# A decoder layer on one Trainium2 core: both folds of cross-attention on parts of the TensorE array, folded keys in two buffers, preparation steps at new places

## The chip, the cores and the metric

The kernel runs on 1 core of one Trainium2 chip. The time is that of one execution on the device, in microseconds (us); three runs of the kernel before gave 1259.86, 1261.22 and 1261.81, a median of 1261.22.

## What is computed

Sixteen sequences (batches) of 512 tokens with 256 channels go through three blocks, each followed by a layer norm of the sum with its input: a linear attention with 16 heads (state = product of two key-value sums), a cross-attention with 16 heads of 64 to 64 context tokens, and a mixture of 8 experts. The second is the one that the change is in:

```python
q = x @ Wq.T
k, v = jnp.split(context @ Wkv.T, 2, axis=-1)
sim = jnp.einsum('bhid,bhjd->bhij', heads(q), heads(k)) * SCALE
attn = jax.nn.softmax(where(mask, sim, max_neg), axis=-1)
out = jnp.einsum('bhij,bhjd->bhid', attn, heads(v))
return merged(out) @ Wout.T + b_out
```

## The kernel before

Each engine runs a program of its own, written out by hand, and they meet at semaphores. A setup computes K and V of all batches and stores them to DRAM. Then a loop goes over the batches (`it`), each in four **slots** of 128 tokens (`pe_slot`, `act_slot`, `dve_slot`, `pool_slot`, `sp_slot`). The iterations run from -2 to 16, so that a batch's inputs are prepared ahead. After the loop come the experts.

Wq is not applied to the tokens: it is folded into the keys, a = Wq.T k ("folded keys", preps A0 to A3, line 440), and Wout into the values, b = v Wout.T ("folded values", preps B0 to B3). In a slot TensorE forms the scores `sim` = t a in two halves of 8 heads, turns the probabilities of the tile before (`pt`, two halves, `pe_pT`), turns the next tokens (`tr`), forms `zb` of the linear attention (`pe_z`), and `ob` = pT b in two halves (`pe_pB`), each behind the low parts `pT_lo` of that half of the turned probabilities. VectorE takes the maximum of each half (`dve_max`), subtracts it (`dve_shift`), ScalarE takes the exponential, VectorE the sum `zsum`, and GpSimd multiplies by its reciprocal.

A product that must be exact is made of three matmuls (lines 137 to 139): each operand is split into a high part, copied by ScalarE in a rounded format (fp32r), and the rest, subtracted by VectorE. An fp32 operand that isn't split goes through TensorE as two matmul instructions in the trace, called passes here (line 440: 16 products a batch are 32 instructions). Before, the folded keys are one such fp32 product per head pair, 128 rows by 128 columns, in which K of the two heads lies on the diagonal of a tile with zeros beside it (`kraw`); the folded values are three matmuls on `vraw`, laid out likewise, whose high part ScalarE makes (line 665) and whose rest GpSimd makes (line 943).

The **preps** of later batches (G and GT: the tokens' Gram matrix and its turned part; B; T1, T0, R, ST: the state of the linear attention; A; SB, SW: its folded weights; Q0, Q1: queries) are steps of TensorE, then ScalarE, then VectorE. The table `ORDER` says in which slot and at which numbered **place** within it each of these three engines does its part. Preps write alternately to two PSUM banks (`pws`); before TensorE starts one, it waits until the one before it on the same bank was taken (`before_on_bank`), and until its operands were (`OPERANDS`: GT reads what ScalarE copied of G). ST is a step of 32 small fp32 products on four tiles of 32x32 of the array (line 416). Places of TensorE: 1 after the first half of `sim`, 2 after the second, 3 after the first half of `pt`, 4 after `tr`, 5 after `zb`, 6 after the second half of `pt`, 7 after the first half of `ob`, 8 after the second.

SP issues the DMAs: K and V of the next batch (`load_kv`, two DMAs each), the mask row into the folded keys, the inputs, and the stores.

## Time and profile before

| what | us |
|---|---|
| profiled execution: its own time | 1261.79 |
| its span, first to last instruction | 1260.1 |
| TensorE busy (matmul) | 1219.2 |
| VectorE busy | 868.0 |
| GpSimd busy | 623.7 |
| ScalarE busy | 567.2 |
| median of three runs | 1261.22 |

The span is that of one execution under the profiler. A busy TensorE counts a matmul from its start to its modelled end, which overlaps the next; the step from start to start is what one costs in a row of them. The granted clock of TensorE is 0.997 of full speed on average. The setup takes about the first 75 us; the `sim` products of the first batch start at 104.52, those of the last batch at 849.41.

### The profile page before, as it was taken

To read this page: it belongs to the slowest core of one execution; us is meant where nothing else is said; L and a number is where in the kernel's file an instruction comes from. 1 tells how busy PE (TensorE), PEld (TensorE's weight loads), DVE (VectorE), ACT (ScalarE), POOL (GpSimd) and SP (SyncE) were. 2 spreads that over 40 slices of the span, in tenths; PEclk is the share of its full clock that TensorE was granted. 3 is DMA by queue.
4 is the path that set the end of the run, shared out by engine and by line. 5 is a ranking of instruction groups with operands and counts; after the bars stand their busy time and mean duration, and the time that the engine had idled before them with its cause. 6 is when DMAs were issued, how large, how long until landed. Compare 5 with 4: busy or idle time off the path is not lost.

```text
span 1260.1 us, 24107 instructions
## 1 busy us (share of the span) xinstructions
PE 1219.2 (97%) x8848; PEld 1100.2 (87%) x8848; DVE 868.0 (69%) x1694; ACT 567.2 (45%) x1117; POOL 623.7 (50%) x986
## 2 busy tenths in 40 slices
PE   8979999999999999999999999988999999999998
PEld 7868889898898898988988989887798899899888
DVE  5557888888888888888888888887533323322435
ACT  2144556555546465556465655555423312421420
POOL 3245766766756767567567575665322112202201
PEclk9999999999999999999999999999999999999999
DMA  9820111102111111111111211220221021022001
GB/s 275 222 74 19 43 35 51 51 26 60 39 39 44 35 51 52 31 56 43 35 49 29 58 45 31 84 81 26 69 92 57 12 67 68 1 68 68 1 1 35
DMA packets 117912, 69.88 MB, mean 55 GB/s; under 512 B 74658, under 2 KB 115363, under 8 KB 117796
## 3 DMA queue, kind: packets, MB, share of 16 engines
q1 hardware_dynamic: 115764, 67.67, 18.3%
q8 instruction: 73, 1.20, 0.4%
q10 hardware_dynamic: 2032, 0.66, 0.2%
q14 instruction: 43, 0.35, 0.1%
HBM read 42.09 MB, written 26.22 MB: 54 GB/s over the span
## 4 chain that ended last, share of the span: by engine, by line
PE 79%; DVE 9%; issue 2%; POOL 1%; ACT 1%; POOLq 0%; DVEq 0%
PE ob L137 7%; PE ob L138 6%; PE ob L139 6%; PE sim L137 6%; PE sim L138 6%; PE sim L139 6%; PE pw L440 4%; PE pw L137 3%; PE pw L138 3%; PE pw L139 3%; PE pt L489 3%; PE pw L390 3%; PE pt L139 2%; PE pt L138 2%; PE pt L137 2%; DVE prob L848 2%
## 5 line engine op out<-in xcount | busy, mean ns | idle before, releaser
L1595 POOL TENSOR_TENSOR w_lo<-w_raw,w_hi 128x2048 fp32r<-128x2048 f32 x16 | 73.7, 4609 | 222.5 <-ACT w_hi L1535 169.3
L137 PE MATMUL ob<-b_hi,pT_hi 128*128 128x256 f32 x512 | 153.3, 299 | 14.6 <-DVE pT_lo L855 14.6
L138 PE MATMUL ob<-b_lo,pT_hi 128*128 128x256 f32 x512 | 144.5, 282 | 0.0
L139 PE MATMUL ob<-b_hi,pT_lo 128*128 128x256 f32 x512 | 144.2, 282 | 0.0
L950 POOL TENSOR_TENSOR prob<-prob,rz 128x512 f32<-128x512 f32 x128 | 130.9, 1044 | 10.4 <-DVE rz L796 10.4
L711 ACT ACTIVATE prob<-prob 128x512 f32<-128x512 f32 x128 | 80.8, 631 | 112.0 <-DVE prob L848 111.4
L843 DVE TENSOR_REDUCE mx<-sim 128x8 f32<-128x512 f32 x128 | 88.2, 689 | 40.1 <-PE sim L139 39.1
L137 PEld LDWEIGHTS ob<-b_hi,pT_hi 128*128 128x128 f32 x512 | 97.5, 190 | 19.4 <-DVE pT_lo L855 18.7
L137 PE MATMUL sim<-a_hi,tT_hi 128*128 128x512 f32 x256 | 103.9, 406 | 0.0
L623 ACT ACTIVATE x<-h,nmr,rstd 128x256 f32<-128x256 f32 x128 | 76.3, 596 | 58.5 <-POOL nmr L869 53.7
L138 PE MATMUL sim<-a_lo,tT_hi 128*128 128x512 f32 x256 | 101.3, 396 | 0.0
L139 PE MATMUL sim<-a_hi,tT_lo 128*128 128x512 f32 x256 | 100.9, 394 | 0.0
L138 PEld LDWEIGHTS ob<-b_lo,pT_hi 128*128 128x128 f32 x512 | 97.7, 191 | 0.7
L139 PEld LDWEIGHTS ob<-b_hi,pT_lo 128*128 128x128 f32 x512 | 97.1, 190 | 0.0
L862 POOL TENSOR_SCALAR ve<-mv 128x1 f32<-128x1 f32 x128 | 27.9, 218 | 130.3 <-DVE mv L759 128.9
L848 DVE TENSOR_TENSOR prob<-sim,mx 128x512 f32<-128x512 f32 x128 | 88.3, 690 | 3.9
L1570 ACT ACTIVATE hT_hi<-zb 128x512 fp32r<-128x512 f32 x30 | 17.7, 591 | 159.8 <-PE zb L139 159.8
L855 DVE TENSOR_TENSOR pT_lo<-pt,pT_hi 128x512 fp32r<-128x512 f32 x128 | 87.3, 682 | 0.4 <-ACT pT_hi L717 0.2
L717 ACT ACTIVATE pT_hi<-pt 128x512 fp32r<-128x512 f32 x128 | 75.6, 591 | 20.7 <-PE pt L489 20.7
L489 PE MATMUL pt<-ident,prob 128*128 128x128 f32 x512 | 78.1, 275 | 3.5 <-DVE pT_lo L855 3.4
L792 DVE TENSOR_REDUCE zsum<-prob 128x16 f32<-128x1024 f32 x64 | 77.7, 1214 | 2.1
L894 POOL TENSOR_TENSOR x<-x,boutbc 128x256 f32<-128x256 f32 x64 | 43.8, 686 | 69.0 <-PE tr L464 62.0
(245 smaller groups left out, 3839.1 us busy)
## 6 DMA issues: line engine op xcount, KB each, us to landing
xraw<-in_x SPq DMA_DIRECT2D x16, 512.0 KB, 3.8
kv_scratch<-stage SPq DMA_DIRECT2D x32, 256.0 KB, 3.1
...
```

The source lines that it names most:

```text
L137: pe.matmul(out, lh, rh, start=first, stop=False)
L138: pe.matmul(out, lh, rl, start=False, stop=False)
L139: return pe.matmul(out, ll, rh, start=False, stop=last)
L489: last = pe.transpose(pt[:, r * P:(r + 1) * P], prob[:, par_n, c:c + P], ident[:, :])
L623: act.activation(dst, src, ACT.Identity, bias=nmr[:, q, ln:ln + 1], scale=rstd[:, q, ln:ln + 1]).then_inc(s[done], 1)
L711: act.activation(prob[:, q, h * HK:(h + 1) * HK], prob[:, q, h * HK:(h + 1) * HK], ACT.Exp).then_inc(s["exp_made"], 1)
L717: act.activation(pT_hi[:, h * 4:h * 4 + 4, :], pt[:, :].rearrange("p (r u) -> p r u", u=P), ACT.Copy).then_inc(s["pt_hi_made"], 1)
L792: dve.tensor_reduce(zsum[:, :], prob[:, q, :].rearrange("p (g j) -> p g j", j=NKV), AX.X, ALU.add).then_inc(s["sum_made"], 1)
L843: dve.tensor_reduce(mx[:, h * 8:h * 8 + 8], by_head(sim[h][:, :]), AX.X, ALU.max).then_inc(s["max_made"], 1)
L848: dve.tensor_tensor(by_head(prob[:, q, h * HK:(h + 1) * HK]), by_head(sim[h][:, :]), mx[:, h * 8:h * 8 + 8].unsqueeze(2).broadcast_to([P, ...
L855: dve.tensor_tensor(pT_lo[:, h * 4:h * 4 + 4, :], pt[:, :].rearrange("p (r u) -> p r u", u=P), f32(pT_hi[:, h * 4:h * 4 + 4, :]), ALU.subt ...
L950: pool.tensor_tensor(part, part, rz[:, q, h * 8:h * 8 + 8].unsqueeze(2).broadcast_to([P, 8, NKV]), ALU.mult).then_inc(s["p_ready"], 1)
```

## The change

- **A on tiles.** `kraw` holds only the 64 values that count, K of 8 heads on array rows 0 to 63 and of the other 8 on rows 64 to 127. A0 and A2 are one stretch on TensorE, A1 and A3 another; each has 16 fp32 products of 64 rows and 64 columns, in turn on the upper and the lower half of the rows, into two banks.
- **B on tiles.** `vraw` is laid out likewise and used as it is, in fp32; the split of V, and that of the turned Wout (`wox`), go. B0 and B1 are one stretch, B2 and B3 another; each has 8 products of 64 rows to 64 output rows with 256 columns, on the four quarters of the array.
- **Two buffers.** The folded keys of even and odd batches have buffers of their own; so has V.
- **Places.** GT goes from slot 1 to slot 0, B2 and B3 to place 1 of slot 1, all of A from slot 3 to slot 2, ST to the end of slot 2 on TensorE and behind h2 of slot 3 on VectorE; SB and SW stay in slot 3; Q1's split on VectorE goes ahead of the first shift of slot 0. VectorE gets a place 1 (ahead of the first maximum) and a place 10 (behind the second `pT_lo`), ScalarE a place 7 (behind `tT_hi`).
- **Loads.** K and V come in one DMA each. In the setup Wkv, Wq and Wout are loaded in pieces, so that the heads lie as the tiles need them.

```diff
-        "B2": ((1, 3), (1, 5), (1, 8)), "B3": ((1, 5), (1, 6), (1, 9)),
-        "A1": ((3, 1), (3, 0), (3, 2)), "A0": ((3, 1), (3, 1), (3, 3)),
+        "B2": ((1, 1), (1, 1), (1, 3)), "B3": ((1, 1), (1, 1), (1, 3)),
+        "A0": ((2, 2), (2, 3), (2, 5)), "A2": ((2, 2), (2, 3), (2, 5)),
...
+    TOGETHER = {"A0": "A2", "A1": "A3", "B0": "B1", "B2": "B3"}
...
+        return a_hi[b % 2][m][:, keys], a_lo[b % 2][m][:, keys]
...
         elif name[0] == "A":
-            need(pe, "k_loaded", 32 * (b + 1))
-            m, hf = i % 2, i // 2
-            for r in range(PAIRS // 2):
-                pr = hf * (PAIRS // 2) + r
-                c = slice(m * P, (m + 1) * P)
-                last = pe.matmul(pw[:, r * P:(r + 1) * P], wqx[:, pr, c], kraw[:, pr, :], start=True, stop=True)
+            need(pe, "k_loaded", 16 * (b + 1))
+            c = slice(i * P, (i + 1) * P)
+            for r in range(PAIRS):
+                for g, mate in enumerate(mates):
+                    d = slice(g * NKV, (g + 1) * NKV)
+                    last = pe.matmul(pws[bank_of(mate)][:, r * NKV:(r + 1) * NKV], wqx[d, r, c], kraw[d, r, :],
+                                     start=True, stop=True)
+                    if r == PAIRS - 1 and g == 0:
+                        last.then_inc(s["prep_made"], 1)
         else:
-            need(pe, "v_hi_made", b + 1)
-            need(pe, "v_lo_made", b + 1)
+            need(pe, "v_loaded", 16 * (b + 1))
             for r in range(2):
-                pr = 2 * i + r
-                last = three_passes(pe, pw[:, r * C:(r + 1) * C], (v_hi[:, pr, :], v_lo[:, pr, :]),
-                                    (wox_hi[:, pr, :], wox_lo[:, pr, :]), True, True)
+                for g, mate in enumerate(mates):
+                    for o in range(2):
+                        d, keys, h = slice(g * NKV, (g + 1) * NKV), slice(o * NKV, (o + 1) * NKV), 2 * (i + r) + o
+                        last = pe.matmul(pws[bank_of(mate)][keys, r * C:(r + 1) * C], vraw[d, q, h, :], wox[d, h, :],
+                                         start=True, stop=True)
+                    if r == 1 and g == 0:
+                        last.then_inc(s["prep_made"], 1)
...
-            act.activation(v_hi[:, :, :], vraw[:, :, :], ACT.Copy).then_inc(s["v_hi_made"], 1)
...
-            pool.tensor_tensor(v_lo[:, :, :], vraw[:, :, :], f32(v_hi[:, :, :]), ALU.subtract).then_inc(s["v_lo_made"], 1)
...
+                    for m in range(MC):
+                        for quarter in range(4):
+                            a, half = quarter // 2, quarter % 2
+                            cols = slice(quarter * C, (quarter + 1) * C)
+                            sp.dma_start(wout_raw[:, m, a * W:(a + 1) * W].rearrange("p (i g d) -> p g i d", g=2, d=NKV)[:, half],
+                                         t["L0_xattn_Wout"][m * P:(m + 1) * P, cols].rearrange("p (i d) -> p i d", d=NKV)
+                                         ).then_inc(loaded["wout"], 16)
```

TensorE in slot 0 before, from `tr` to the second half of `pt`:

```order
L464 MATMUL tr<-ident,xraw 128x128 x2
L390 MATMUL pw<-xraw 128x257 x4
L390 MATMUL pw<-xraw 128x129 x4
L516 MATMUL zb<-zw_hi,qT_hi 128x384
L517 MATMUL zb<-zw_lo,qT_hi 128x384
L518 MATMUL zb<-zw_hi,qT_lo 128x384
L516 MATMUL zb<-zw_hi,qT_hi 128x384
L517 MATMUL zb<-zw_lo,qT_hi 128x384
L518 MATMUL zb<-zw_hi,qT_lo 128x384
L489 MATMUL pt<-ident,prob 128x128 x4
```

And the same stretch of the changed kernel:

```order
L472 MATMUL tr<-ident,xraw 128x128 x2
L392 MATMUL pw<-xraw 128x257 x4
L392 MATMUL pw<-xraw 128x129 x4
L524 MATMUL zb<-zw_hi,qT_hi 128x384
L525 MATMUL zb<-zw_lo,qT_hi 128x384
L526 MATMUL zb<-zw_hi,qT_lo 128x384
L524 MATMUL zb<-zw_hi,qT_hi 128x384
L525 MATMUL zb<-zw_lo,qT_hi 128x384
L526 MATMUL zb<-zw_hi,qT_lo 128x384
L395 MATMUL pw<-ident,g_sb 128x128
L497 MATMUL pt<-ident,prob 128x128 x4
```

GT (`pw<-ident,g_sb`) now stands between `zb` and `pt` in the slot in which G (`pw<-xraw`) is made; it stood in slot 1, between the halves of `sim`.

VectorE from the end of slot 2 into slot 3 before: the second `pT_lo` of slot 2, h1 and its statistics, ST's products `s`, h2 and its statistics, and in slot 3 the first maximum, with the splits of A (`a_lo`) behind it:

```order
L855 TENSOR_TENSOR pT_lo<-pt,pT_hi 128x512
L832 SCALAR_TENSOR_TENSOR h<-zb,rstd,xb 128x256
L757 BN_STATS bst<-h 128x6
L759 BN_AGGR mv<-bst 128x2
L747 SCALAR_TENSOR_TENSOR s<-bkq,r_sb,pw 128x32 x4
L773 TENSOR_TENSOR h<-ob,x 128x256
L757 BN_STATS bst<-h 128x6
L759 BN_AGGR mv<-bst 128x2
L843 TENSOR_REDUCE mx<-sim 128x8
L730 TENSOR_TENSOR a_lo<-pw,a_hi 128x512
L848 TENSOR_TENSOR prob<-sim,mx 128x512
```

And of the changed kernel:

```order
L860 TENSOR_TENSOR pT_lo<-pt,pT_hi 128x512
L734 TENSOR_TENSOR a_lo<-pw,a_hi 128x512 x2
L837 SCALAR_TENSOR_TENSOR h<-zb,rstd,xb 128x256
L761 BN_STATS bst<-h 128x6
L763 BN_AGGR mv<-bst 128x2
L777 TENSOR_TENSOR h<-ob,x 128x256
L761 BN_STATS bst<-h 128x6
L763 BN_AGGR mv<-bst 128x2
L751 SCALAR_TENSOR_TENSOR s<-bkq,r_sb,pw 128x32 x4
L848 TENSOR_REDUCE mx<-sim 128x8
L853 TENSOR_TENSOR prob<-sim,mx 128x512
```

Two splits of A stand ahead of h1 in slot 2, and ST's products stand behind h2, ahead of slot 3's first maximum.

## Rows read from the trace of the kernel before

**Rows 1.** Page, busy us (share) x instructions.
```profile
PE 1219.2 (97%) x8848; PEld 1100.2 (87%) x8848; DVE 868.0 (69%) x1694; ACT 567.2 (45%) x1117; POOL 623.7 (50%) x986
```

**Rows 2.** Waits of TensorE: total us, times, longest.
```profile
PE ob L137 <- DVE pT_lo L855: 14.6, 19, 1.3
```

**Rows 3.** Timeline, TensorE, one batch: start us, length us, what, [idle before].
```profile
604.18 0.40 PE L137 MATMUL sim<-a_hi,tT_hi 128*128 128x512 f32 x1
...
611.53 0.60 PE L489 MATMUL pt<-ident,prob 128*128 128x128 f32 x4
...
616.23 0.40 PE L137 MATMUL sim<-a_hi,tT_hi 128*128 128x512 f32 x1
...
628.98 0.40 PE L137 MATMUL sim<-a_hi,tT_hi 128*128 128x512 f32 x1
...
631.78 0.60 PE L489 MATMUL pt<-ident,prob 128*128 128x128 f32 x4
...
637.33 0.39 PE L137 MATMUL ob<-b_hi,pT_hi 128*128 128x256 f32 x1 [0.77 <-DVE pT_lo L855]
...
638.85 0.39 PE L137 MATMUL sim<-a_hi,tT_hi 128*128 128x512 f32 x1
...
654.43 0.40 PE L137 MATMUL sim<-a_hi,tT_hi 128*128 128x512 f32 x1
```

**Rows 4.** Timeline, VectorE, slot 0 (first row) and slot 2.
```profile
608.51 0.74 DVE L728 SCALAR_TENSOR_TENSOR qT_lo<-pw,bq,qT_hi 128x512 fp32r<-128x512 f32 x1
...
629.18 0.42 DVE L773 TENSOR_TENSOR h<-ob,x 128x256 f32<-128x256 f32 x1 [0.20 <-PE ob L139]
...
630.58 0.69 DVE L843 TENSOR_REDUCE mx<-sim 128x8 f32<-128x512 f32 x1 [0.30 <-PE sim L139]
...
634.10 1.22 DVE L792 TENSOR_REDUCE zsum<-prob 128x16 f32<-128x1024 f32 x1
...
636.60 0.68 DVE L855 TENSOR_TENSOR pT_lo<-pt,pT_hi 128x512 fp32r<-128x512 f32 x1
637.19 0.47 DVE L832 SCALAR_TENSOR_TENSOR h<-zb,rstd,xb 128x256 f32<-128x256 f32 x1
...
638.26 0.70 DVE L747 SCALAR_TENSOR_TENSOR s<-bkq,r_sb,pw 128x32 f32<-128x32 f32 x4
```

**Rows 5.** Timeline, TensorE: values' fold with its follower, keys' fold with its follower.
```profile
613.39 0.28 PE L137 MATMUL pw<-wox_hi,v_hi 128*128 128x256 f32 x1
...
614.80 0.28 PE L137 MATMUL ob<-b_hi,pT_hi 128*128 128x256 f32 x1
...
643.43 1.05 PE L440 MATMUL pw<-kraw,wqx 128*128 128x128 f32 x8
644.32 0.60 PE L489 MATMUL pt<-ident,prob 128*128 128x128 f32 x4
```

**Rows 6.** Timeline, TensorE, around the state products (ST) of slot 2.
```profile
633.53 0.34 PE L518 MATMUL zb<-zw_hi,qT_lo 128*128 128x384 f32 x1
633.79 0.76 PE L416 MATMUL pw<-wk,t_sb 128*32 128x32 f32 x64
634.49 0.66 PE L489 MATMUL pt<-ident,prob 128*128 128x128 f32 x4
```

**Rows 7.** Timeline, weight loads of TensorE, in the feed-forward part.
```profile
910.43 0.57 PEld L1693 LDWEIGHTS pw<-ident,lgT 8*128 8x128 f32 x8 [0.35 <-issue]
```

**Rows 8.** Timeline, ScalarE, slot 0 (two rows) and slot 3.
```profile
610.14 0.57 ACT L684 ACTIVATE tT_hi<-tr 128x512 fp32r<-128x512 f32 x1
...
612.66 0.49 ACT L617 ACTIVATE g_hi<-pw 128x386 fp32r<-128x386 f32 x1
...
644.52 0.60 ACT L618 ACTIVATE a_hi<-pw 128x512 fp32r<-128x512 f32 x1
```

**Rows 9.** Groups by line and shape, GpSimd: total us, mean ns, idle before.
```profile
L943 POOL TENSOR_TENSOR v_lo<-vraw,v_hi 128x1024 fp32r<-128x1024 f32 x16 | 38.0, 2377 | 0.0
```

**Rows 10.** Timeline, SP's queue, in the setup.
```profile
37.89 0.59 SPq L1226 DMA_DIRECT2D wout_raw<-in_L_xattn_Wout  x1
```

More of the change, by code:

```diff
@@ L308, in setup_and_attention, with folded_keys @@
     counted = {}
-    half = lambda buf, h: buf[:, :, h * HK:(h + 1) * HK]
+    def folded_keys(b, m, h):
+        keys = slice(h * HK, (h + 1) * HK)
+        return a_hi[b % 2][m][:, keys], a_lo[b % 2][m][:, keys]
     def sp_slot(sp, it, slot, e):
@@ L361, in x_tiles @@
         return t["x"][bass.ds(b, 1), :, :].rearrange("o (i p) c -> p (o i) c", p=P)
-    def load_kv(sp, dst, which, b, sem):
-        for h in range(2):
-            q = slice(64 * h, 64 * h + 64)
-            if isinstance(b, int):
-                src = kv_scr[which, b, q, :, :]
-            else:
-                src = kv_scr[which, bass.ds(b, 1), q, :, :].rearrange("o p r j -> (o p) r j")
-            sp.dma_start(dst[q, :, 64 * h:64 * h + 64], src).then_inc(s[sem], 16)
     def pe_prep(pe, name, it, q):
+        if name in TOGETHER.values():
+            return
         b = batch_of(name, it)
         pw = pws[bank_of(name)]
+        mates = (name, TOGETHER[name]) if name in TOGETHER else (name,)
         latest = {}
-        for back, other in [before_on_bank(it, name)] + [(0, x) for x in OPERANDS.get(name, ())]:
+        for back, other in [before_on_bank(it, x) for x in mates] + [(0, x) for x in OPERANDS.get(name, ())]:
             if other:
@@ L542, in pe_slot @@
         n = 4 * it + slot
-        prep = lambda place: [pe_prep(pe, x, j, par(0)) for x, j in at("pe", slot, place, it)]
+        prep = lambda place: [pe_prep(pe, x, j, par(it - j)) for x, j in at("pe", slot, place, it)]
         if has_sim:
@@ L776, in dve_slot @@
             dve_stats(dve, 2, n - 2, q, h2[:, q, :])
+        prep(1)
         if has_sim:
@@ L1010, in setup_and_attention @@
     x1 = k.sb("x1", [P, 2, TPB, C + 1])
-    a_hi = k.sb("a_hi", [P, MC, KEYS], F32R)
-    a_lo = k.sb("a_lo", [P, MC, KEYS], F32R)
+    a_odd = [k.sb(f"a_{part}", [P, MC, KEYS], F32R) for part in ("hi", "lo")]
     b_lo = k.sb("b_lo", [P, PAIRS, C], F32R)
-    v_hi = k.sb("v_hi", [P, PAIRS, P], F32R)
-    v_lo = k.sb("v_lo", [P, PAIRS, P], F32R)
+    vraw = k.sb("vraw", [P, 2, PAIRS, NKV])
+    k.sb("w2_hi1_room", [P, PAIRS, P])
+    a_even_hi = k.sb_over("hT_lo1_room", "a_even_hi", [P, MC, KEYS])
+    a_hi = ([a_even_hi[:, m, :] for m in range(MC)], [a_odd[0][:, m, :] for m in range(MC)])
+    a_lo = ([k.sb_over(room, f"a_even_lo{m}", [P, KEYS])[:, :] for m, room in enumerate(("x2T_lo_room", "w2_hi1_room"))],
+            [a_odd[1][:, m, :] for m in range(MC)])
     prob = k.sb("prob", [P, 2, KEYS])
@@ L1218, in _ @@
                 if n == 6:
-                    sp.dma_start(wqx[:, :, 1:C + 1], t["L0_xattn_Wq"].rearrange("(i p) c -> p i c", p=P)).then_inc(loaded["wqx"], 16)
+                    for half in range(2):
+                        sp.dma_start(wqx[half * NKV:(half + 1) * NKV, :, 1:C + 1], wq_halves[half]).then_inc(loaded["wqx"], 16)
                 if n == 8:
```

83 lines of the change are left out of this document (40 added, 43 removed), and 24 rows, old and new, of tables (FIRST_ORDER, ORDER).

## The prediction

> **What bounds the kernel now.** I read the page first: TensorE is busy 97% of the span [rows 1]. That share alone doesn't say what sets the pace, so next comes the table of waits: TensorE's largest one is for the low parts of the turned probabilities, VectorE's `pT_lo`, 14.6 us in 19 waits [rows 2]. Then the timeline of TensorE over one batch. One batch is four slots; a slot begins with the first `sim` product. The starts are 604.18, 616.23, 628.98, 638.85 and 654.43 [rows 3], so the slots take 12.05, 12.75, 9.87 and 15.58 us and the batch 50.25 us; batches 1 to 13 all take this to 0.02 us. Slots 0, 1 and 3 have no wait over 0.1 us in that timeline: TensorE's own work fills them. Slot 2 is VectorE's: the second half of `ob` starts only at 637.33 after 0.77 us of idleness for `pT_lo` [rows 3]. The change takes TensorE's work from slot 3 and spreads it, so what matters is how long each slot would be for TensorE and how long for VectorE.
>
> **VectorE's chain in a slot,** from slot 2, where it decides (times from the slot's start, 628.98) [rows 4]: the sum h2 and its statistics from 0.20 take 1.10 (the first maximum at 1.60 waited 0.30 for `sim`); the sum of the probabilities starts at 5.12, the second `pT_lo` at 7.62 (2.50 later) and runs 0.68, and `ob`'s second half starts at 8.35. After `pT_lo` (a step of 0.59) come h1 and its statistics, 1.07, then the state products `s` (ST), 0.70 and a gap, together 0.75. So any VectorE work put ahead of the maximum moves 8.35 back one for one, unless it fits before 1.60. With the last half of `ob`, 12 products of 0.118 or 1.42 us, no slot is shorter than 9.77.
>
> **The change part by part.**
> 1. Folded keys (A): now 4 stretches of 4 fp32 products, each in two passes. Eight passes take 643.43 to 644.32, 0.89 us [rows 5], so 0.111 a pass of 128 columns and 3.56 us a batch. They become two stretches (A0 with A2, A1 with A3) of 16 products, 32 passes of 64 columns, half on array rows 0 to 63 and half on 64 to 127.
> 2. Folded values (B): 4 stretches of 6 products; two of them take 613.39 to 614.80, 1.41 us [rows 5]. They become two stretches of 8 products, 16 passes of 256 columns on four 64x64 tiles.
> 3. What a stretch on tiles costs isn't in the trace; the nearest row is ST, which already uses four tiles of 32x32 [rows 6]. Its 64 passes span 0.76, less the 0.20 of the last one's own length: about 0.59 with its stream, 9.2 ns a pass, against 0.111/4 = 27.8 ns for 32 columns alone. So tiles do run together, three or four at a time. Around it: the `zb` product before starts at 633.53 and streams 0.17, ST starts at 633.79 (0.09 lost), the transposes behind at 634.49 (0.10 lost), and four of them take 0.66 where four elsewhere take 0.60 [rows 3, 6]. In all 0.25 us to enter and leave tiles. For B I take 4 groups of four passes at 0.222 plus 0.25: 1.14. For A, 16 groups of two: the stream is 0.055, but each needs a weight load of 128 columns; eight such loads with almost no stream behind them span 0.57 less 0.14, so 0.062 each [rows 7]. 16 x 0.062 + 0.25 = 1.24. Bounds: no switching cost gives 0.89 for both; no overlap of tiles gives 16 x 0.222 + 0.25 = 3.8 for B and 32 x 0.062 + 0.25 = 2.2 for A. I take 1.24 and 1.14 because ST is the same data type, engine and place, and differs only in size.
> The Trainium skill (TensorE: Matmul & The Clock Gate, LDWEIGHTS) gives a load as its columns over 1.2 GHz, 107 ns for 128. The row above shows 62 ns, so the trace disagrees; by the page A would be 16 x 0.107 + 0.25 = 1.96 a stretch.
> 4. Slot 0: 12.05, plus the transpose GT that comes here from slot 1 (0.11, a fourth of a row of four transposes), less 1.41 - 1.14 = 0.27 for B. GT stands behind `zb` and reads G, which ScalarE copies only after `tT_hi` (place 7). Now `tT_hi` starts at 5.96 [rows 8]; the low part of Q1, 0.7 us [rows 4], moves ahead of the first shift and so delays both exponentials: 6.66, +0.50 for `tT_hi`, +0.9 for the two copies of G (the first alone is 0.49 [rows 8]): 8.06. TensorE is through with `zb` at 7.35 (611.53 [rows 3]). A new wait of 0.71, behind it both `pT` and `ob`. Slot 0: 12.60.
> 5. Slot 1: 12.75 - 0.11 (GT) - 0.27 (B2, B3) = 12.37. VectorE has two more splits ahead of its second maximum, but T1 (1.40) stands on TensorE ahead of the second `pt`, so that is ready at 7.25, VectorE at about 6.7: hidden, by 0.5. Without that cover it would cost what exceeds 0.5.
> 6. Slot 2: both `sim` end at 2.80 (631.78 [rows 3]); A0, A2 at 4.04. ScalarE starts the copy 0.20 behind (644.52 against 644.32 [rows 5, 8]) and takes 0.60: 4.84; VectorE two splits of 0.60: 6.07; first `pT_lo` to 6.75; TensorE, free at 5.99, resumes at 6.80. It reaches A1, A3's end at 6.80 + 0.44 + 1.42 + 1.24 = 9.90; VectorE from the sum at 6.75: +2.50, +0.73 = 9.98. `ob` 1.42 and ST 0.84: slot 2 ends at 12.24, 2.37 more than now. VectorE still has to split A1 and A3 (copy 10.10 to 10.70, splits from 10.73, h1 at 11.93, free at 13.00), 0.76 into slot 3.
> 7. Slot 3: h2 from 0.76, 1.10, then ST's products 0.75: first maximum at 2.61 instead of 1.60, so the second `ob` starts at 8.35 + 1.01 = 9.36; TensorE would be there at 15.58 - 3.56 (A) - 2.80 (Q) - 1.42 = 7.8. Then 1.42, and Q0, Q1, 12 products like the two `sim`: 2.80. 13.58, against 15.58.
> Sum: 12.60 + 12.37 + 12.24 + 13.58 = 50.79, or **+0.54 us a batch**, 13 x 0.54 = 7.0; batch 0 some +0.5, batch 14 (no G, T, Q) nothing.
> 8. Costed at nothing: GpSimd's v_lo, 38.0 us in all [rows 9], and ScalarE's v_hi go. Neither ended a wait of TensorE, so nothing is late in their stead. The K and V loads become one DMA each and are issued a batch ahead. The second buffer for the folded keys removes A's wait on the running `sim`; no row shows such a wait.
> 9. Setup: 12 more DMA issues on SP (Wkv 4, wqx 1, Wout 7). The seven for Wout, 0.59 each [rows 10], stand 4.1 us ahead of the store of a K/V product; four staging buffers at one product every 1.36 us cover most. Between 0 and +4, I take +1. In the first, `sim`-free pass the paired A save up to 2 and ST comes later; four copies of ScalarE go in setup: -2 to +1, I take -1. Net 0.
> The profiled execution took 1261.8 us (span 1260.1); 1261.8 + 7.5 = 1269.3. The median of the runs is 0.6 lower: **1269**.
>
> **The rivals.**
> *Tiles without switching cost (faster).* If the gaps of 0.25 lie under other work, each stretch is 0.25 shorter. Slots 0 and 1 follow one for one, slots 2 and 3 together by twice as much: 1.0 a batch, so -0.46, 13 x 0.46 = 6: about 1255. It decides from stretches shorter by 0.54/4 = 0.135, that is 1.10 for A and 1.00 for B. For it: the body alone is 0.89 to 0.99. Against: all three gaps stand around ST in every batch.
> *Two passes of a product in line.* If B's tiles run two at a time, because both passes of a product go to one tile in turn, B takes 8 x 0.222 + 0.25 = 2.03: +0.89 in slots 0 and 1, +24 in all: 1293. ST's 9.2 ns a pass speaks against it; its tiles share no rows, B's do.
> *Weight loads in turn.* If the loads of A's two tiles don't overlap, A takes 32 x 0.062 + 0.25 = 2.23, +0.99 twice in each of 14 batches, +28: 1297. ST speaks against it: 9.2 ns a pass, load included, where a load of 32 columns alone would be 0.062/4 = 15.5 ns.
> By the length that the Trainium skill (TensorE: Matmul & The Clock Gate, LDWEIGHTS) gives, with loads of the two tiles side by side, the price is +0.72 twice a batch, +20, or 1289; the 62 ns speak against it.
> *Nothing gained, nothing lost.* If the tiles cost what A and B cost now, or VectorE has 0.5 more slack in slots 2 and 3, about 1262.
>
> **How the numbers follow.** A measurement of this kernel tells 0.2%, some 2.5 us, from no change. Forecast (1263 to 1277): 0.48. No switching cost, or more slack (1252 to 1259): 0.28. Near zero: 0.12. Slow tiles of either kind: 0.12. Faster 0.29, same 0.15, slower 0.56. The range takes in the free switch and reaches to the two-at-a-time tiles: 1254 to 1292; the forecast's own is 1263 to 1277.
>
> **What would show it.** Slots of about 12.6, 12.4, 12.2 and 13.6 us; GT waiting 0.7 for ScalarE's copy of G; the first `pT` of slot 2 waiting 0.8, the second `ob` of slot 3 1.7 for VectorE; A at 1.2 and B at 1.1 a stretch. It is wrong if slot 3 is under 13, or if the A and B stretches are under 1.0 or over 1.6.

## The result, and the profile after

The changed kernel takes **1302.44 us** (median of 4 runs, 1300.08 to 1302.67) against 1261.51 of the kernel before; the ratio is 1.0322 (95% interval 1.0304 to 1.0340). It is slower by 41 us, where 8 were forecast, and outside the range (1254 to 1292). One execution of the run `one_load` took 3241.38 us and is left out of its numbers below; in every other run the executions lie within 8 us of each other.

The page of the changed kernel, busy time by engine, answers to [rows 1]:
```profile
PE 1235.1 (95%) x9488; PEld 1072.8 (82%) x9488; DVE 862.0 (66%) x1694; ACT 556.9 (43%) x1097; POOL 586.6 (45%) x968
```
TensorE is busy 16 us longer in a span that is 40.5 longer, so most of the loss is TensorE standing still. Its waits, the table that answers to [rows 2]:
```profile
PE pt L497 <- DVE pT_lo L860: 28.9, 36, 1.5
PE pw L395 <- ACT g_sb L626: 6.2, 14, 1.3
...
PE pw L428 <- POOL sbdT L919: 4.6, 1, 4.6
...
PE pw L442 <- DVE t_sb L740: 2.2, 1, 2.2
PE pw L442 <- DVE a_even_lo L734: 2.0, 1, 2.0
```
The first row is for the most part two waits in each batch (slots 2 and 3), the second one a batch (GT's wait for the copy of G). The three with "1" in the second column stand in the first pass, before any sim.

Timeline of TensorE over one batch, answering to [rows 3] and [rows 5] (a slot's first sim, and what stands beside the tile stretches):
```profile
637.93 0.40 PE L137 MATMUL sim<-a_even_hi,tT_hi 128*128 128x512 f32 x1
...
647.80 0.28 PE L139 MATMUL ob<-b_hi,pT_lo 128*128 128x256 f32 x1
648.01 1.09 PE L452 MATMUL pw<-wox,vraw 64*64 64x256 f32 x16
649.03 0.38 PE L137 MATMUL ob<-b_hi,pT_hi 128*128 128x256 f32 x1
649.26 0.28 PE L138 MATMUL ob<-b_lo,pT_hi 128*128 128x256 f32 x1
...
650.55 0.40 PE L137 MATMUL sim<-a_even_hi,tT_hi 128*128 128x512 f32 x1
...
662.90 0.47 PE L137 MATMUL sim<-a_even_hi,tT_hi 128*128 128x512 f32 x1
...
665.53 0.40 PE L139 MATMUL sim<-a_even_hi,tT_lo 128*128 128x512 f32 x1
665.86 2.00 PE L442 MATMUL pw<-kraw,wqx 64*128 64x64 f32 x32
667.79 0.66 PE L497 MATMUL pt<-ident,prob 128*128 128x128 f32 x4
...
670.55 0.63 PE L497 MATMUL pt<-ident,prob 128*128 128x128 f32 x4 [0.62 <-DVE pT_lo L860]
...
676.75 0.50 PE L137 MATMUL sim<-a_even_hi,tT_hi 128*128 128x512 f32 x1
...
682.64 0.63 PE L497 MATMUL pt<-ident,prob 128*128 128x128 f32 x4 [0.93 <-DVE pT_lo L860]
```
The slots take 12.62 (12.54 in most other batches), 12.35, 13.86 and (to 690.15) 13.4 us. In batches 1 to 12 the batch is 52.14 to 52.22, against 50.25 before. The stretch of folded keys (L442) starts 0.10 behind the end of sim's stream (665.76) and the transposes follow at 667.79: 2.03 us. The stretch of folded values (L452) goes from the end of ob's stream (647.92) to 649.03, and the product behind it takes 0.23 instead of 0.12: 1.22. In slot 3 TensorE waits 0.93 ahead of the second half of `pt`, for the `pT_lo` of the first.

Timeline of VectorE in the same slot 2 and the start of slot 3:
```profile
668.52 1.29 DVE L734 TENSOR_TENSOR a_lo<-pw,a_hi 128x512 fp32r<-128x512 f32 x2 [1.14 <-ACT a_hi L626]
669.73 0.68 DVE L860 TENSOR_TENSOR pT_lo<-pt,pT_hi 128x512 fp32r<-128x512 f32 x1
...
675.19 1.29 DVE L734 TENSOR_TENSOR a_lo<-pw,a_hi 128x512 fp32r<-128x512 f32 x2 [1.69 <-ACT a_hi L626]
676.39 0.47 DVE L837 SCALAR_TENSOR_TENSOR h<-zb,rstd,xb 128x256 f32<-128x256 f32 x1
...
677.54 0.42 DVE L777 TENSOR_TENSOR h<-ob,x 128x256 f32<-128x256 f32 x1
```
Twice VectorE stands still for a copy of folded keys, and each time the work that a slot waits for is queued behind the split.

**Where the 40.5 us of the two spans lie.** The first sim comes at 119.30 instead of 104.52: 14.8. From there to the start of the last batch's last slot it is 804.5 instead of 778.8: 25.7. Behind that both kernels take 376.7.

Within the 14.8, three parts can be told from the timelines. The first `zb` comes at 78.81 instead of 75.88: 2.9. From there to the first `zb` of slot 2 it is 10.75 (89.56) instead of 7.69 (83.57): 3.1. From that to the first sim it is 29.74 instead of 20.95: 8.8. The second part is G and GT, after and before:
```profile
79.96 4.47 PE L392 MATMUL pw<-xraw 128*128 128x257 f32 x16
...
85.98 0.30 PE L395 MATMUL pw<-ident,g_sb 128*128 128x128 f32 x1 [1.33 <-ACT g_sb L626]
```
```profile
77.01 2.79 PE L390 MATMUL pw<-xraw 128*128 128x257 f32 x16
...
81.36 0.30 PE L393 MATMUL pw<-ident,g_sb 128*128 128x128 f32 x1 [0.28 <-ACT g_sb L618]
```
G takes 1.7 longer because in this execution it runs at the lower clock; in the profiles of st_first, a_swapped, a_8rows, one_load and a_plain, with the same steps, it takes 2.79. The other 1.4 is GT, which at its new place waits for ScalarE's copy of G.

The third part runs for most of its time at TensorE's lower clock. The windows of the changed kernel (columns: stretch, length, busy of five engines, granted clock, DMA share, GB/s):
```profile
80.20:83.20 3.00, 3.00 (x9) 2.35 (x8) 1.66 (x5) 0.00 (x0) 0.94 (x3) 0.50 0.39 147
...
98.00:101.00 3.00, 1.14 (x12) 0.95 (x10) 1.21 (x2) 1.16 (x3) 0.00 (x0) 0.50 0.50 175
...
113.00:116.00 3.00, 2.91 (x8) 2.05 (x9) 1.02 (x2) 0.90 (x2) 1.82 (x3) 0.50 0.00 0
```
and of the kernel before:
```profile
95.00:98.00 3.00, 3.00 (x17) 2.65 (x15) 0.69 (x1) 0.93 (x2) 2.92 (x6) 0.56 0.00 0
98.00:101.00 3.00, 2.02 (x13) 1.57 (x12) 1.84 (x4) 1.63 (x4) 2.71 (x2) 0.87 0.01 1
```
A clock of 0.50 is 1.2 GHz. Before, it lasts 3.4 us in all (by these two windows); now it covers G and most of 98 to 117 (107 to 110 is at 0.92). Ahead of each fall TensorE had stood still: 2.0 us before the first `zb`, 2.2 before the first folded-key stretch, and then in the 4.6 for `sbdT`.

### The profile page after: what moved, and what is told of

Same layout as the page of the kernel before. It is cut to its first block, busy times and chain, and to the rows that moved or that the text cites. A ratio compares the mean times of both kernels' runs of the same rounds, so it can differ in the third digit from the quotient of the medians.

```text
span 1300.6 us, 25250 instructions
## 1 busy us (share of the span) xinstructions
PE 1235.1 (95%) x9488; PEld 1072.8 (82%) x9488; DVE 862.0 (66%) x1694; ACT 556.9 (43%) x1097; POOL 586.6 (45%) x968
## 4 chain that ended last, share of the span: by engine, by line
PE 65%; DVE 18%; ACT 5%; issue 4%; POOL 1%; DVEq 0%; POOLq 0%
PE ob L137 6%; PE ob L138 6%; PE ob L139 6%; PE sim L137 5%; PE sim L138 5%; PE sim L139 5%; PE pw L442 5%; DVE prob L853 3%; DVE mx L848 3%; PE pw L452 2%; PE pt L139 2%; PE pt L138 2%; PE pt L137 2%; PE pt L497 2%; PE pw L137 2%
## 5 line engine op out<-in xcount | busy, mean ns | idle before, releaser
L497 PEld LDWEIGHTS pt<-ident,prob 128*128 128x128 f32 x512 | 58.6, 140 | 49.5 <-issue 40.1
L871 POOL TENSOR_TENSOR rstd<-ve,epsc 128x1 f32<-128x1 f32 x128 | 71.9, 561 | 10.7
L1827 DVE SCALAR_TENSOR_TENSOR hT_lo<-sim,hT_hi 128x512 fp32r<-128x512 f32 x62 | 42.8, 691 | 44.3 <-ACT hT_hi L1585 44.3
L442 PEld LDWEIGHTS pw<-kraw,wqx 64*128 64x128 f32 x1024 | 62.1, 194 | 12.1 <-issue 5.5
```

Of the source, the lines that this page charges most:

```text
L442: last = pe.matmul(pws[bank_of(mate)][:, r * NKV:(r + 1) * NKV], wqx[d, r, c], kraw[d, r, :], start=True, stop=True)
L497: last = pe.transpose(pt[:, r * P:(r + 1) * P], prob[:, par_n, c:c + P], ident[:, :])
```

## The experiments

Times are medians, of four executions unless said otherwise, beside 1261 to 1262 for the kernel before in every set. "The pair" is two folds on array tiles side by side. "First sim" and slots are of the profiled run.

### What sets the pace of a folded-key stretch

**a_swapped**
```diff
-  pe.matmul(pws[...][:, r * NKV:(r + 1) * NKV], wqx[d, r, c], kraw[d, r, :], ...)
+  pe.matmul(pws[...][0:NKV, (r % 4) * P:(r % 4 + 1) * P], kraw[d, r, :], wqx[d, r, c], ...)
```


> The folded keys' products with their operands exchanged: the raw keys are the weights (64 rows by 64 columns), the slice of Wq is the moving operand (128 columns, before 64); each product writes 64 partitions. It is a measurement of cost: the folded keys come out turned, so the output is not the reference's. Theory L (an fp32 pass of A takes 0.111 us because its weight load has 128 columns, whatever streams behind it): with half the load and twice the stream a pair of passes falls from 0.111 to about 0.056, a stretch from 1.93 to about 1.05 us; slot 2, which has two stretches, falls from 13.87 to about 12.2, and the kernel by 14 x 1.6 + about 2 in the first pass, from 1302 to about 1278. Rival W (the price is that of 64-row tiles or of entering and leaving them): the stretch stays within 0.1 of 1.93 and the time at about 1302. Rival M (what streams sets it): the stretch grows, and the time with it.

Measured: 1299.23, a stretch's first to last start 1.70 instead of 1.73, slot 2 13.79. Nothing of what theory L expected. But the run was badly chosen: it took the load from 128 to 64 columns and the stream from 64 to 128.

**a_half_keys**
```diff
-  pe.matmul(pws[...][:, r * NKV:(r + 1) * NKV], wqx[d, r, c], kraw[d, r, :], ...)
+  pe.matmul(pws[...][:, r * NKV:r * NKV + NKV // 2], wqx[d, r, c], kraw[d, r, 0:NKV // 2], ...)
```


> The folded keys' products with only the first 32 of the 64 keys streamed, the weights unchanged (64 rows by 128 columns): the other half of the folded keys is not computed. It is a measurement of cost. Theory L (weight load): nothing is gained, a stretch stays at 1.93 us and the kernel at 1302 within 2. Rival M (what streams sets it): a pair of passes falls by up to 0.05, a stretch to about 1.1 to 1.2, the kernel to about 1280.

Measured: 1299.97, stretch 1.70, slot 2 13.80. What streams is not what sets the pace at 64 columns.

**a_64x64**
```diff
-  pe.matmul(pws[...][:, r * NKV:(r + 1) * NKV], wqx[d, r, c], kraw[d, r, :], ...)
+  pe.matmul(pws[...][0:NKV, r * NKV:(r + 1) * NKV], kraw[d, r, :], wqx[d, r, i * P:i * P + NKV], ...)
```


> The folded keys' products with weights of 64 columns and 64 streamed columns at once (raw keys as weights, half of the slice of Wq streamed); it measures cost, half of the folded keys is not computed and the rest comes out turned. Of the two runs before, one halved the stream (32 columns, load 128) and one halved the load (64 columns) but doubled the stream to 128, and both left a pair of passes at 0.110; a stream of 128 fp32 columns alone is 0.107 in a row of the kernel before, so the exchanged run could not tell the load from the stream. Theory L2 (a pair takes the longer of load and stream, each 0.107 at 128 columns): now both are 64 columns, the pair falls to about 0.055, a stretch from 1.73 to about 0.9, slot 2 from 13.86 to about 12.2, the kernel from 1302 to about 1278. Rival F (a fixed interval of 0.11 between two fp32 passes of one 64-row tile, or 0.055 to issue each): stretch 1.70, time about 1300.

Measured: **1273.83**, stretch 0.93, slot 2 12.16. Timelines of TensorE, one stretch each of a_swapped, a_half_keys and a_64x64:
```profile
661.49 1.97 PE L442 MATMUL pw<-wqx,kraw 64*64 64x128 f32 x32
```
```profile
664.69 1.98 PE L442 MATMUL pw<-kraw,wqx 64*128 64x32 f32 x32
```
```profile
693.97 1.15 PE L442 MATMUL pw<-wqx,kraw 64*64 64x64 f32 x32
```
Load 64 with stream 128 and load 128 with stream 32 give the same; only both at 64 halve it. A pair of fp32 passes takes the longer of its load and its stream, each about 0.11 us at 128 columns. In the changed kernel the two weight loads of a pair start 0.006 us apart, and so do the two passes, so the tiles work side by side; the next pair follows 0.11 later. So the change halved the streamed columns and gained nothing by it, since the load still has 128. And slot 2 fell by 1.70 where its two stretches got shorter by 1.6: they stand on the path one for one.

**a_8rows** and **a_transpose**
```diff
-  pe.matmul(pws[...][:, r * NKV:(r + 1) * NKV], wqx[d, r, c], kraw[d, r, :], ...)
+  pe.matmul(pws[...][:, r * NKV:(r + 1) * NKV], wqx[e8, r, c], kraw[e8, r, :], ...)   # a_8rows: 8 rows of d
+  pe.transpose(pws[...][:, r * NKV:(r + 1) * NKV], wqx[d, r, c], ident[d, d])         # a_transpose
```


> The folded keys' products with only 8 of their 64 rows (8x128 weights, 64 columns streamed), so most of each sum is left out; it measures cost. It asks why the row that the estimate used, 8 loads of 8x128 at 0.062 each, was no guide to the 0.110 of these. Theory R (a load of 128 columns is cheap where it has few rows): a pair falls to about 0.065, a stretch from 1.73 to about 1.0, the kernel to about 1276. Rival N (rows don't matter, the difference is between a transpose and a product): the stretch stays at 1.7, the kernel at 1300.

> The folded keys' products replaced by transposes of the same slices of Wq (64x128 as weights, 64 columns of the identity streamed, one pass each where a product takes two); nothing of the keys is computed; it measures cost. Theory N (a transpose's load is cheap): a pair of transposes takes about 0.062, a stretch of 16 spans 7 x 0.062 = 0.43. Rival R (a load of 64 rows and 128 columns takes 0.107 in a transpose as well): it spans 7 x 0.11 = 0.77.

Measured: 1302.04 with 8 rows (two executions), 1260.75 with transposes (eight, 1257.23 to 1262.56). Timelines of TensorE, of a_8rows, and of a_transpose with its weight loads:
```profile
664.13 2.00 PE L443 MATMUL pw<-kraw,wqx 8*128 8x64 f32 x32
```
```profile
642.62 0.71 PE L442 MATMUL pw<-ident,wqx 64*128 64x64 f32 x16
```
```profile
642.61 0.57 PEld L442 LDWEIGHTS pw<-ident,wqx 64*128 64x128 f32 x16
```
The number of rows changes nothing (2.00 as before). Two transposes side by side come every 0.06, the price of [rows 7]. So the load of 128 fp32 columns costs half as much in a transpose as in a pass of a product, and the estimate had taken its price from transposes.

### Tiles or places

**a_plain**
```diff
-    TOGETHER = {"A0": "A2", "A1": "A3", "B0": "B1", "B2": "B3"}
+    TOGETHER = {"B0": "B1", "B2": "B3"}
...
-            for r in range(PAIRS):
-                for g, mate in enumerate(mates):
...
+            for r in range(PAIRS // 2):
+                pr = hf * (PAIRS // 2) + r
+                last = pe.matmul(pw[:, r * P:(r + 1) * P], wqx[:, pr, c], kraw[:, pr, :], start=True, stop=True)
```
(kraw again block-diagonal and loaded in two halves, the keys' half of Wkv and Wq loaded whole; the buffers stay double.)

> The changed kernel with all its places, only the folded keys not on tiles: each as in the kernel before (8 passes of 128x128, 0.89 us, raw keys block-diagonal), the two of a former pair one behind the other. Theory (a stretch on tiles takes 2.13 with what surrounds it and does no more than two plain ones of 0.89): slot 2 has two such stretches and falls from 13.86 by 2 x 0.35 = 0.7 to 13.2, the other slots stay, a batch is 51.4; with the shorter first pass (the copy of A0 needs not wait for A2's end) the kernel at 1285 to 1292. Rival (tiles and plain passes cost the same, the places alone make the loss): 1300 within 3.

Measured: **1273.66**, slots 12.54, 12.35, 12.78, 13.00, first sim 112.5. The fall is 28.8 us, where 10 to 17 were expected: slot 2 by 1.08, slot 3 by 0.39, together 22.1 in the loop, and the first sim comes 6.8 earlier (of which 1.7 is G at full clock). Timelines of TensorE and VectorE in its slot 2 (which starts at 540.04):
```profile
542.90 1.95 PE L443 MATMUL pw<-kraw,wqx 128*128 128x128 f32 x16
544.68 0.60 PE L495 MATMUL pt<-ident,prob 128*128 128x128 f32 x4
```
```profile
544.62 0.69 DVE L732 TENSOR_TENSOR a_lo<-pw,a_hi 128x512 fp32r<-128x512 f32 x1
545.51 0.69 DVE L732 TENSOR_TENSOR a_lo<-pw,a_hi 128x512 fp32r<-128x512 f32 x1 [0.20 <-ACT a_hi L624]
546.12 0.68 DVE L858 TENSOR_TENSOR pT_lo<-pt,pT_hi 128x512 fp32r<-128x512 f32 x1
```
Two plain stretches of 8 take 1.78 where the pair takes 2.03. And the first is done 0.89 before the second, so its copy and split run beside the second's products; the pair hands over both at its end. Hence pT_lo starts 6.08 into the slot and not 6.83.

**old_places**
```diff
-        "A0": ((2, 2), (2, 3), (2, 5)), "A2": ((2, 2), (2, 3), (2, 5)),
-        "A1": ((2, 7), (2, 8), (2, 10)), "A3": ((2, 7), (2, 8), (2, 10)),
+        "A0": ((3, 1), (3, 1), (3, 3)), "A2": ((3, 1), (3, 1), (3, 3)),
+        "A1": ((3, 6), (3, 8), (3, 9)), "A3": ((3, 6), (3, 8), (3, 9)),
```
(and all other steps, first pass included, as before; SB and SW ahead of the second pair.)

> The folds on tiles, double buffers and loads as changed, but every step at the place of the kernel before (both folded-key pairs in slot 3, ST and GT where they stood, the first pass too). Theory T (the loss per batch is in what a folded-key stretch costs, not in the places): a batch is 50.25 - 0.54 (folded values) + 0.5 (two stretches of 2.03 for 3.56) = 50.2, the first sim at about 110, the kernel at about 1264. Rival P (the places cost the 1.9 a batch by VectorE's chain): then the same 50.2, but it says that of the 1.9 a batch nearly all is the places'; the two differ in the new places' slots 2 and 3, where a stretch in TensorE's free time would have cost nothing. If a batch is over 51 here, the tiles cost more than their own stretches.

Measured: **1349.29**, slots 12.00, 13.17, 9.86, 20.12. A miss of both theories. Waits of TensorE:
```profile
PE pw L440 <- DVE zw_lo L732: 34.8, 15, 2.4
```
A pair writes two banks at once, so it waits for the splits of both steps before it, here SB's and SW's: up to 2.4 us in each batch, and the kernel has more half-clock time (mean clock 0.967). At the places of the single stretches the pairs cost far more than at those of the change. The comparison meant for this run is made by a_plain and h4.

**h1**: a_plain with every place of the kernel before (B0 with B1 and B2 with B3 still on tiles).

> The folded values on tiles as changed; the folded keys as in the kernel before (8 passes of 128x128, raw keys block-diagonal) but double-buffered; all places those of the kernel before. Theory: a batch is 50.25 - 2 x 0.27 = 49.7, the first sim at about 106 (Wkv's values in halves and Wout in pieces), the kernel at 1262 - 7.6 + 1 = about 1255. If the folded values' saving isn't on the path, 1262.

Measured: 1268.95, slots 12.00, 13.18, 9.86, 15.55. A miss. In slot 0, in the same place as before, the folded values on tiles save 0.05 and not 0.27. In slot 1 they wait:
```profile
PE pw L448 <- issue: 8.8, 14, 0.8
```
The view names no releaser, but in the batch looked at (from 509.47) the first load of each pair follows 0.07 us behind ScalarE's copy of the step that holds one of its two banks: 518.90 behind the copy of G (518.33 and 0.50), 525.55 behind that of GT (525.21 and 0.27). In slot 1 that costs 0.62 us, in slot 0 the stretch starts 0.25 behind the product before it instead of 0.09.

### VectorE and ScalarE in slots 2 and 3

**split_behind**
```diff
-        "A1": ((2, 7), (2, 8), (2, 10)), "A3": ((2, 7), (2, 8), (2, 10)),
+        "A1": ((2, 7), (2, 8), (3, 0)), "A3": ((2, 7), (2, 8), (3, 0)),
```


> The changed kernel with one VectorE place moved: the split of A1 and A3 stands behind h1 and its statistics (start of slot 3) instead of ahead of them (end of slot 2). In the changed kernel's slot 2 VectorE idles 1.69 us for ScalarE's copies of A1 and A3, and h1 (1.15 with its statistics) and h2 of slot 3 stand behind it. Theory V (VectorE's start of slot 3 sets that slot, as the prediction's steps 6 and 7 have it): h1 fills that idle time, h2 starts about 1.1 earlier, TensorE's wait of 0.93 in slot 3 goes, slot 3 falls from 13.40 to about 12.4, the kernel from 1302 to about 1289. Rival T (slot 3 is TensorE's own work): within 2 of 1302.

Measured: 1291.52, slot 3 12.74 instead of 13.40, all others unchanged. VectorE at the end of its slot 2:
```profile
563.02 0.47 DVE L837 SCALAR_TENSOR_TENSOR h<-zb,rstd,xb 128x256 f32<-128x256 f32 x1
...
564.79 1.29 DVE L734 TENSOR_TENSOR a_lo<-pw,a_hi 128x512 fp32r<-128x512 f32 x2 [0.62 <-ACT a_hi L626]
565.99 0.42 DVE L777 TENSOR_TENSOR h<-ob,x 128x256 f32<-128x256 f32 x1
```
The idle time of 1.69 is 0.62, h1 lies in it, and h2 starts 13.49 into slot 2's time instead of 14.64. Theory V holds, though only 0.66 of the 1.15 reach the end of slot 3. The rest is lost on the way: `s` waits 0.15 for ScalarE's sums, and the first maximum (568.04, 1.68 into the slot instead of 2.43) can't start before the first half of `sim` is done. TensorE still waits 0.27 for `pT_lo`.

**h2**: h1 with one step moved.
```diff
-        "A1": ((3, 1), (3, 0), (3, 2)), ...
+        "A1": ((2, 7), (2, 8), (3, 2)), ...
```


> Beside h1 (folded values on tiles, folded keys as before but double-buffered, old places; 1268.95, slots 12.00, 13.18, 9.86, 15.55) one step moved: the products of A1 stand in slot 2, ahead of the second half of ob (place 7, its copy at ScalarE's 8), its VectorE split where it was. The second buffer is what allows it. Theory: 0.89 us leave slot 3, and in slot 2 they fill the 0.77 that TensorE waits there for pT_lo: slots 9.98 and 14.66, 0.77 a batch, the kernel at about 1258. Rival: ScalarE's copy or the bank holds up slot 2 or 3, no gain, 1269.

Measured: 1270.35, slots 12.00, 13.18, 9.86, 15.86. In slot 2 the stretch cost nothing at all, as expected. Slot 3 grew, with 0.89 less to do. ScalarE and VectorE at the end of slot 2:
```profile
543.35 0.60 ACT L622 ACTIVATE a_hi<-pw 128x512 fp32r<-128x512 f32 x1 [1.49 <-PE pw L441]
543.85 0.50 ACT L649 ACTIVATE acc<-acc,bvsum 128x256 f32<-128x256 f32 x1
```
```profile
545.94 0.72 DVE L747 SCALAR_TENSOR_TENSOR s<-bkq,r_sb,pw 128x32 f32<-128x32 f32 x4 [1.75 <-ACT acc L649]
546.58 0.42 DVE L773 TENSOR_TENSOR h<-ob,x 128x256 f32<-128x256 f32 x1
```
The copy of A1 stands ahead of ScalarE's four sums for ST and waits 1.49 for its products; the sums are late by as much, s waits for them, and h2 and slot 3's first maximum stand behind s. In slot 3 TensorE now waits 0.47 for `s` and 0.41 for `pT_lo`.

**h3**: h2 with B2 and B3 at place 1 of slot 1 and GT behind them at place 3.

> Beside h2 the steps of slot 1 in another order: B2 and B3 between the two sims (place 1, as in the change), GT behind them (place 3). In h1 the pair B2, B3 waits 0.62 us in slot 1, since it needs both banks and GT's copy and B1's split stand ahead. Theory: that wait goes and slot 1 falls from 13.18 to 12.45 (the changed kernel's 12.35 and 0.11 for GT); with slots 12.00, 9.98 and 14.66 a batch of 49.1, and the kernel at about 1248, below both. Rival: GT now holds up T1 or T0 through GpSimd's g_lo, slot 1 over 12.9 and the kernel over 1254.

Measured: 1270.56, slot 1 13.24. The wait for the banks went, but TensorE now waits 0.40 for pT_lo in slot 1. The rival's size without its mechanism: it is VectorE, not GpSimd. Here T1 stands at place 7, so nothing covers the pair's two splits, which is the case that step 5 of the prediction named.

**h4**: h2 with A1's copy behind the sums, and slots 0 and 1 in the change's order except for Q1's split.
```diff
-        "A1": ((2, 7), (2, 8), (3, 2)), ...
+        "A1": ((2, 7), (3, 0), (3, 2)), ...
...
-        "GT": ((1, 1), (1, 3), (1, 3)), "B2": ((1, 3), (1, 5), (1, 8)), "B3": ((1, 3), (1, 5), (1, 8)),
+        "GT": ((0, 5), (0, 7), (0, 8)), "B2": ((1, 1), (1, 1), (1, 3)), "B3": ((1, 1), (1, 1), (1, 3)),
...
-        "T1": ((1, 7), (1, 8), (1, 9)), ...
+        "T1": ((1, 5), (1, 8), (1, 10)), ...
```


> Folded values on tiles, folded keys as before (8 passes of 128x128) and double-buffered. A1's products in slot 2 ahead of the second half of ob, but its copy on ScalarE behind the four sums for ST (slot 3, place 0) as in the kernel before: in h2 the copy stood ahead of those sums, 1.49 us of ScalarE idle, so ST's s on VectorE began 1.75 late and slot 3 grew from 15.55 to 15.86. Slots 0 and 1 in the change's places (GT in slot 0, B2 and B3 between the sims, T1 at 5), but Q1's split where it was (place 5), since its earlier place should be what delays G's copy. Theory (only waits were in the way of h2 and h3): slots about 12.2, 12.35, 9.86 and 14.7, a batch of 49.1, the kernel at about 1246 to 1251, below both kernels. Rival: VectorE's own work in slot 3 has no room either, slot 3 at 15.3 or more, the kernel over 1258.

Measured: **1247.11**, ratio 0.9886 (0.9869 to 0.9902): 1.1% faster than the kernel before, and faster than the change, slots 12.17, 12.35, 9.94, 14.66, a batch 49.12. Timeline of TensorE, the start of a batch, A1's stretch, the start of slot 3 and that of the next batch:
```profile
499.70 0.39 PE L137 MATMUL sim<-a_even_hi,tT_hi 128*128 128x512 f32 x1
...
531.72 1.05 PE L441 MATMUL pw<-kraw,wqx 128*128 128x128 f32 x8
...
534.16 0.40 PE L137 MATMUL sim<-a_even_hi,tT_hi 128*128 128x512 f32 x1
...
548.82 0.40 PE L137 MATMUL sim<-a_hi,tT_hi 128*128 128x512 f32 x1
```
Slot 0 is 0.37 shorter than in the change: with Q1's split back at place 5, GT's wait is gone.

### The first pass

**st_first**: ST ahead of the folded keys in the first pass.
```diff
+        "ST": ((3, 1), (3, 0), (3, 2)),
         "A0": ((3, 1), (3, 1), (3, 2)), "A2": ((3, 1), (3, 1), (3, 2)),
         "A1": ((3, 3), (3, 3), (3, 5)), "A3": ((3, 3), (3, 3), (3, 5)),
-        "ST": ((3, 4), (3, 0), (3, 8)), "SB": ((3, 5), (3, 8), (3, 8))}
+        "SB": ((3, 5), (3, 8), (3, 8))}
```


> Only the first pass (batch 0's preparation, before any sim) changed: ST stands ahead of the folded keys again, as in the kernel before, instead of behind them. Theory S (the first pass is longer by 8.8 us because ST comes last: GpSimd's chain behind it, 4.6 us of TensorE waiting, and the half clock that follows the idle time): the first sim moves from 119.3 to about 112, the kernel from 1302 to about 1295. Rival (the loads in pieces, or the half clock of the folded keys on tiles by itself, make it late): within 2 of 1302.

Measured: 1302.94, first sim 118.95. Theory S falls: `s` was ready at 96, and TensorE still waited 5.3 us for `sbdT`.

**one_load**: Wkv, Wq and Wout in whole DMAs, as in the kernel before.

> Wkv, Wq and Wout each loaded in whole DMAs as in the kernel before (12 issues fewer on SP), without the reordering of rows and columns, so the heads are mixed up and the output is not the reference's; all else as changed. Theory: of the 14.8 us that the first sim is later, the 2.9 that stand before the first zb come from the pieces: the first zb returns from 78.8 to about 76, the kernel from 1302 to about 1299. Rival (they hide behind the staging buffers, as the prediction had it): within 1 of 1302.

Measured: 1297.88 (three executions: 1296.81, 1297.88, 1302.21); the first zb at 75.87 instead of 78.81. But one profile does not give the size: in the others with the change's loads the first zb comes at 77.16 to 79.02 (a_swapped, a_transpose), without them at 75.51 to 75.88 (setup_both, the kernel before). So the pieces cost 1.3 to 3.5 us ahead of the first zb; the medians (4.6 apart, with executions up to 5.4 apart) tell it no closer.

**first_behind**
```diff
-        "A0": ((3, 1), (3, 1), (3, 2)), "A2": ((3, 1), (3, 1), (3, 2)),
-        "A1": ((3, 3), (3, 3), (3, 5)), "A3": ((3, 3), (3, 3), (3, 5)),
-        "ST": ((3, 4), (3, 0), (3, 8)), "SB": ((3, 5), (3, 8), (3, 8))}
+        "ST": ((3, 4), (3, 0), (3, 8)),
+        "A0": ((3, 4), (3, 3), (3, 8)), "A2": ((3, 4), (3, 3), (3, 8)),
+        "A1": ((3, 6), (3, 8), (3, 9)), "A3": ((3, 6), (3, 8), (3, 9))}
```


> Only the first pass changed: ST ahead of the folded keys, and the folded keys behind slot 3's zb product (places 4 and 6) instead of ahead of it (1 and 3). The run with ST alone moved gained nothing: TensorE still waited 5.3 us for GpSimd's sbdT, which stood in GpSimd's queue behind the statistics of that zb product. Theory Z (no sim runs there, so folded keys ahead of zb hold zb's statistics, GpSimd's chain and sbdT back by two stretches with the copies and splits between them): the wait for sbdT goes, the first sim moves from 119.3 to 110 to 113, the kernel from 1302 to about 1294. Rival C (the half clock alone makes the first pass long): within 2 of 1302.

Measured: 1298.48 (1296.06 to 1303.08), 4.0 less than the change, half of what was expected. Waits of TensorE between 78 and 118 us:
```profile
PE pw L444 <- DVE s L753: 3.1, 1, 3.1
PE pw L430 <- DVE a_even_lo L736: 2.0, 1, 2.0
```
The 4.6 for sbdT is gone, so theory Z names a true cause; in its place stand the pair's waits for both banks.

**setup_both**: one_load and first_behind together.

> The changed kernel with two edits of the first pass together: the loads in whole DMAs (first zb 2.9 us earlier; heads mixed up, so not the reference's output) and ST and the folded keys behind slot 3's zb (4.3 us earlier in one profile, though one pass's clock varies). If the two are separate parts of the 14.8 us, they add: first sim at about 112, the kernel at 1302 - 2.9 - 4.3 = about 1295. If the rest is the pair's need of both banks and the half clock, the first sim stays over 109, against 105 to 107 where the folded keys are single (h1, h2, h3).

Measured: 1296.46, that is 6.0 less than the change. Whether the two parts add can't be told from the medians, since 4.0 and the loads' part are each known only to some 2 us.

What the pair itself costs in the first pass shows when the profiles are set side by side, in the three parts of the result section (us):

| | folded keys | to the first zb | from there to slot 2's zb | from there to the first sim |
|---|---|---|---|---|
| before | single, behind slot 3's zb | 75.88 | 7.69 | 20.95 |
| h4 | single, behind | 76.60 | 10.71 | 21.55 |
| a_plain | single, ahead | 77.22 | 9.07 | 26.24 |
| first_behind | pairs, behind | 77.30 | 10.74 | 26.96 |
| setup_both | pairs, behind | 75.51 | 10.68 | 28.38 |
| change | pairs, ahead | 78.81 | 10.75 | 29.74 |

The middle column is 7.69 with GT at its old place, 9.07 at its new one, and up to 1.7 more where G ran at the lower clock; that is chance of the execution, and one reason why the first sim differs by 4 us between profiles of the same first pass (119.3 in the change, 118.3 in split_behind, 115.4 in a_8rows). The last column is steadier (29.74 in one_load and split_behind too, 28.69 in a_8rows). There the pairs cost 2.5 to 3.5 us more than single stretches where both stand ahead of slot 3's zb, and 5.4 to 6.8 where both stand behind it; the place ahead costs single stretches 4.7 and pairs 0.3 to 2.8. These are single profiles. How the pair's part divides between its waits for two banks and the longer half clock was not separated.

## Why the prediction was wrong

**The forecast's side was right, its size was not.** Of the steps:

1. *A stretch of folded keys 1.24 (step 3).* **This step failed.** It is 2.03 in slot 2. "16 x 0.062" took the price of a weight load from [rows 7], a row of transposes; in passes of a product it is 0.11 (a_half_keys, a_8rows), and replacing the passes by transposes on the same tiles brings the 0.06 back (a_transpose). Slot 2 has two stretches, so it was to be 2 x 0.79 longer than forecast: 12.24 + 1.58 = 13.82, measured 13.86. This alone is 14 x 1.6 = 22 us, an estimate. With it the sum would have been 1291, still inside the range; the setup (step 9 of the prediction, point 7 here) took it out.
The Trainium skill (TensorE: Matmul & The Clock Gate, LDWEIGHTS) gives a load as its columns over 1.2 GHz, whatever the rows, an estimate of 107 ns for 128; the passes of products agree (0.110 to 0.112, with 8 rows too), the transposes do not (0.06). The prediction named the 1.96 a stretch that follow from the Trainium skill, an estimate, and held the row against it. The row was of another kind of instruction, and the stretch measured 2.03.
2. *Weight loads in turn (a rival, 1297).* The right size by the wrong mechanism: the loads of the two tiles do run side by side (those of a pair start 0.006 apart, and a pair of passes takes what one takes), but each takes twice what was assumed.
3. *Folded values 1.14 a stretch.* 1.22 measured; four tiles of 64x64 do run abreast. *Two passes of a product in line*, the rival against it, is refuted.
4. *Slot 0, 12.60, with GT waiting 0.71 for ScalarE.* 12.54 to 12.62. The cause is as named: in h4, with Q1's split at its old place, the wait is gone. The number is partly luck: the wait is 0.38 and not 0.71, and GT (0.20 instead of 0.11), the restart behind the wait (0.15) and the folded values (1.22) cost more than forecast.
5. *Slot 1, 12.37.* 12.35; VectorE's two splits are hidden, and h3 shows that without T1 ahead they are not.
6. *Slot 3, 13.58, set by VectorE.* 13.40, and split_behind shows that VectorE sets it. Of its two causes named, the split of A1 and A3 is shown; s ahead of the maximum wasn't tried alone. The wait itself stood elsewhere: no 1.7 ahead of the second `ob`, but 0.93 ahead of the second half of `pt`, a wait that the prediction's slot 3 doesn't have. The second `ob` starts 9.08 into the slot (9.36 forecast).
7. *Setup, net 0 (step 9).* **This failed too:** +14.8. "+1" for the DMA issues was 2.9 in this profile (1.3 to 3.5 over all), and stood in the first zb, not where Wout's pieces are. GT's new place, which step 4 costed for slot 0 of the loop, was put at nothing in the first pass, where it takes 1.4; 1.7 more is G at the lower clock, which not every execution has. "-1" for the paired folded keys and the later ST was wrong in sign, it is +8.8: the keys stood ahead of slot 3's zb, whose statistics and sbdT wait behind them on GpSimd (first_behind, 4.0 in the medians), and the pairs cost 2.5 to 6.8 more than single stretches there. The step counted TensorE's work and not who waits behind it.
8. *What was not in the sum at all:* a pair needs two banks and hands its two results over together. a_plain shows it: 1.08 less in slot 2 where the stretches alone give 0.5. Step 6 does have VectorE's two splits one behind the other, but not that single stretches would let the first begin earlier.

So the sum closes: 22 for the stretches and 14.8 for the first pass, added to the forecast of 1269, make 1306; the loop gives back some 4 of it (25.7 where 7.5 and 22 would be 29.5), more than half of that in slot 3, 0.18 a batch shorter than forecast. That leaves the measured 1302. The prediction's own signs said it too: stretches of folded keys over 1.6 were to show it wrong.

Against the kernel before, the tiles of the folded keys cost 28.8 us (change to a_plain; the whole loads of the keys' half of Wkv and of Wq in a_plain are part of it and weren't timed alone), and the rest of the change 12. Per batch that is 1.5 and 0.4 of the 1.9.
